# Gathers issued one tile further ahead of the scatter-adds, and a reordered VectorE step, in an attention and expert kernel

## The reference

```python
x = x + xattn(layernorm(x), ctx, Wq, bq, Wk, bk)          # (16, 56, 512), ctx (16, 1500, 512)
# in the expert layer, x is layernorm(x) as 896 rows of 512:
scores = sigmoid(x @ gate_w.T) + bias                     # 16 experts
topk_w, topk_idx = top_k(scores, 4); topk_w /= sum(topk_w)
z  = silu(x @ Wg[e].T) * (x @ Wu[e].T)                    # 256 wide, for each expert
out = sum_e (z * cw[:, e]) @ Wd[e].T + silu(x @ Sg.T) * (x @ Su.T) @ Sd.T
```

## Time and profile before

| | us |
|---|---|
| median of three runs | 559.57 |
| lowest, highest | 557.12, 560.98 |
| the profiled execution's own time | 557.56 |
| its span, first to last instruction | 555.8 |
| busy in it: TensorE matmuls | 487.7 (88%) |
| VectorE, ScalarE, GpSimd | 260.6 (47%), 156.6 (28%), 118.8 (21%) |

### The profile page before, as it was taken

The page is one execution under the profiler, slowest core; times in us unless marked ns, Lnnn a source line. Parts: engine busy times, 40 slices in busy tenths (PEclk is TensorE's granted clock), DMA queues, the critical chain, the costliest instruction groups (busy, mean ns, idle before and its releaser), DMA issues.

```text
span 555.8 us, 10809 instructions
## 1 busy us (share of the span) xinstructions
PE 487.7 (88%) x2472; PEld 297.6 (54%) x2473; DVE 260.6 (47%) x707; ACT 156.6 (28%) x303; POOL 118.8 (21%) x100
## 2 busy tenths in 40 slices
PE   3999999999999999997997935899998889899960
PEld 1583445363636363633475623677766666576740
DVE  3204336273736354544358634354656456654520
ACT  0000302020202020302122431345555456444430
POOL 1000000000000000000002221454554446335531
PEclk9969999999999999998999968799999899899995
DMA  9999999999999999999454654866758677555542
GB/s 216 401 421 423 384 424 418 410 425 401 428 401 426 402 425 403 422 427 404 154 169 97 170 153 153 278 164 149 190 115 214 194 199 180 101 90 93 109 59 36
DMA packets 28231, 149.04 MB, mean 268 GB/s; under 512 B 4072, under 2 KB 4200, under 8 KB 16424
## 3 DMA queue, kind: packets, MB, share of 16 engines
q1 hardware_dynamic: 15832, 123.08, 55.7%
q0 software_dynamic: 8720, 20.21, 20.2%
q10 hardware_dynamic: 3664, 5.57, 3.2%
HBM read 133.84 MB, written 15.01 MB: 268 GB/s over the span
## 4 chain that ended last, share of the span: by engine, by line
PE 66%; DMA 14%; issue 9%; DVE 3%; ACT 2%; DVEq 2%; POOL 2%; POOLq 1%; ACTq 0%; SPq 0%
PE b L571 15%; PE scores L547 15%; PE b L677 14%; DMA taken<-h_rows,take_at 8%; PE b L535 6%; DMA out<-y_sb,add_at 4%; PE b L497 4%; PE scores L677 2%; PE scores L509 2%; PE b L561 2%; DMA w_qk<-in_wk 1%; DVEq L323 1%; PE b L584 1%; PE b L516 1%; ACT probs_t L828 1%
## 5 line engine op out<-in xcount | busy, mean ns | idle before, releaser
L571 PE MATMUL b<-ctx_rows,probs_t 125*64 125x512 f32 (+1 forms) x384 | 86.3, 600 | 0.0
L547 PE MATMUL scores<-ctx_cols,g_t 128*64 128x500 f32 x384 | 84.8, 586 | 0.0
L459 POOL DMA_INDIRECT out<-y_sb,add_at x34 | 53.7, 1579 | 88.3 <-ACT add_at L928 52.6
L423 POOL TENSOR_TENSOR rstd<-var_eps,neg_half 128x1 f32<-128x1 f32 x16 | 8.8, 551 | 268.2 <-DVE var_eps L1019 268.2
L677 PE MATMUL b<-w_hi,taken_hi 128*128 x136 | 57.9, 426 | 1.1 <-ACT taken_hi L905 1.1
L677 PE MATMUL b<-w_lo,taken_hi 128*128 x136 | 56.1, 412 | 0.0
L1277 DVE TENSOR_TENSOR w_lo<-w_raw,w_hi (+1 forms) x33 | 39.7, 1223 | 29.1 <-ACT w_hi L894 29.1
L571 PEld LDWEIGHTS b<-ctx_rows,probs_t 125*64 125x64 f32 (+1 forms) x384 | 26.4, 138 | 48.2 <-issue 47.3
L547 PEld LDWEIGHTS scores<-ctx_cols,g_t 128*64 128x64 f32 x384 | 26.3, 137 | 48.3 <-issue 48.3
L497 PE MATMUL b<-cst,taken 128*128 128x128 f32 x164 | 26.6, 287 | 25.1 <-DMA taken<-h_rows,take_at 24.1
L444 POOL DMA_INDIRECT taken<-h_rows,take_at x34 | 43.1, 1268 | 12.9 <-issue 9.7
(11 more groups left out here) (213 smaller groups left out, 674.1 us busy)
## 6 DMA issues: line engine op xcount, KB each, us to landing
ctx_rows<-in_ctx SPq DMA_DIRECT2D x48, 1024.0 KB, 15.4
ctx_cols<-in_ctx_t SPq DMA_DIRECT2D x32, 1500.0 KB, 18.6
w_raw<-in_experts SPq DMA_DIRECT2D x11, 1536.0 KB, 7.1
h_rows<-h ACTq DMA_DIRECT2D x16, 115.5 KB
taken<-h_rows SPq DMA_DIRECT2D x7, 264.0 KB, 3.0
out<-xs ACTq DMA_DIRECT2D x2, 784.0 KB
shared_raw<-in_shared SPq DMA_DIRECT2D x1, 1536.0 KB, 32.5
xs<-in_x ACTq DMA_DIRECT2D x12, 112.0 KB
```

The lines of the kernel that those rows point to most:

```text
L459: nc.gpsimd.indirect_dma_start(out[:, :], bass.IndirectOffsetOnAxis(ap=add_at[i][:, 0:1], axis=0), y_sb[:, i * DIM:(i + 1) * DIM], None, c ...
L547: last = nc.tensor.matmul(scores[HALF * b:HALF * (b + 1), n, 0:CHUNK], g_t[:, k, HALF * b:HALF * (b + 1)], ctx_cols[:, at:at + CHUNK], sta ...
L571: last = nc.tensor.matmul(b3[HALF * b:HALF * (b + 1), :], probs_t[0:rows_in(p), at:at + HALF], ctx_rows[0:rows_in(p), g, b, c * DIM:(c + 1 ...
```

## The change

GpSimd issues `gather(9)` and `gather(10)` ahead of `add_shared(5)`, `gather(7)` and `gather(8)` ahead of `add_shared(4)`, and in the loop `gather(t+5)` ahead of `add(t)`, where it was `gather(t+4)`. VectorE's step takes the low half, the weight column and the row numbers of coming tiles between `gated_rows` and `z_rows`. TensorE does `ranks` earlier and `lay_tables` later, and VectorE casts `plan` ahead of the fourth shared tile's two gate steps.

```diff
             add_shared(3)
-            add_shared(4)
             pool.wait_ge(init_stored, 16)
             pool.wait_ge(h_stored, PAIRS * 32 + 16)
             pool.wait_ge(plan_ready, 1)
             n_inner = inner_pairs(pool)
             gather(SHARED, 1)
             gather(SHARED + 1, 0)
+            add_shared(4)
+            gather(SHARED + 2, 1)
+            gather(SHARED + 3, 0)
             add_shared(5)
-            gather(SHARED + 2, 1)
+            gather(SHARED + 4, 1)
             add_shared(6)
-            gather(SHARED + 3, 0)
-            with pool.Fori(0, n_inner) as pair:
+            with pool.Fori(0, n_inner - 1) as pair:
                 for k in range(2):
                     t = pair * 2 + (SHARED + k)
-                    gather(t + 4, 1 - k)
+                    gather(t + 5, k)
                     add(t, 1 - k)
-            t = n_inner * 2 + SHARED
-            for k in range(4):
+            t = n_inner * 2 + (SHARED - 2)
+            gather(t + 5, 0)
+            for k in range(6):
                 add(t + k, 1 - k % 2)
...
# TensorE
             up_hi(2, 0, shared_hi, shared_lo, 0)
+            ranks(last_pair)
             z_transpose(1)
             up_lo(2, 0, shared_hi, 0)
             shared_transpose(3)
             down(1, 1, shared_hi, shared_lo, 0)
-            ranks(last_pair)
...
             z_transpose(3)
-            lay_tables()
             up_lo(4, 0, shared_hi, 0)
             shared_transpose(5)
+            lay_tables()
             down(3, 1, shared_hi, shared_lo, 0)
...
# VectorE
             def silu_rows(t, i):
                 gate_rows(t, i)
+                weigh_rows(t, i)
+
+            def weigh_rows(t, i):
                 dve.wait_ge(w_ready, t - (SHARED - 1))
                 settle(dve)
                 dve.wait_ge(gated_ready, t + 1)
...
             pick(last_pair)
+            weigh(last_pair)
             z_to_lo(1)
-            weigh(last_pair)
+            rank_rows(last_pair)
             shared_silu(2)
             taken_to_lo(3)
-            rank_rows(last_pair)
             z_to_lo(2)
...
             enter(last_pair)
+            dve.wait_ge(table_rows_ready, 1)
+            nc.vector.tensor_copy(plan[:], scores[0:1, 2, 0:TABLES * TILES]).then_inc(plan_ready, 1)
             shared_silu(4)
             taken_to_lo(5)
-            dve.wait_ge(table_rows_ready, 1)
-            nc.vector.tensor_copy(plan[:], scores[0:1, 2, 0:TABLES * TILES]).then_inc(plan_ready, 1)
             z_to_lo(4)
...
             def step(t, i):
                 z_to_lo(t - 1)
-                silu_rows(t, i)
+                gate_rows(t, i)
                 taken_to_lo(t + 1)
                 take_weight(t + 1, 1 - i)
                 name_take(t + 3, 1 - i)
+                weigh_rows(t, i)
                 more_thirds(t + 1)
```

## The result

The change makes the kernel slower by 0.9%: 565.69 us (median of 8 runs, 564.04 to 568.89) against 561.21 (8 runs, the three of the table above among them, 557.12 to 569.14), a ratio of 1.0087 with an interval of 1.0046 to 1.0128. Forecast were 534 us. The profiled execution took 565.78 us, 8.2 more than the one before.

A forecast was written before the change was run, and what follows sets the result against it. TensorE was taken to set the pace wherever fed, with late gathers starving it. From 557.6 us profiled, 18.0 for the entry and 6.7 for the loop leave 532.9; as the profiled run lies 2.0 under the median, 534, range 527 to 541.

The forecast's parts named there:

- The entry: Start up to expert tile 11: earlier plan and gathers bring tile 11 18 us earlier, bounds 15 to 21.
- VectorE's new step: no cost, with little cover.: Loop: z_rows ends 2.3 us behind taken_hi, 0.3 us of cover left; cost 0, bounds 0 and 10 us.
- VectorE's order binds: Rival, loop: cover short by 0.3 to 0.5 us in most steps, 10 to 15 us back, 543 to 549; chance 0.13.
- The scatter-adds ... Cost 0: Loop: scatter-adds leave some 2 us later, hidden by 1.3 us before keep_y's need and ScalarE's idle time; cost 0.
- the loop's gain of 6.7: Loop: gathers issued ahead of scatter-adds are seldom late, 6.7 us gained, between 3 and 9.
- this rival: Rival, loop: scatter-adds hold ScalarE, binding over 6.9 us of landing; slower, up to 568 us; chance 0.05.
- the 155 to 160 forecast: Sign, loop: tile 11 to tile 40 would take 155 to 160 us.
- The prediction's own mechanism: GpSimd cannot write descriptors while VectorE holds the port pair; by this each add up to 1.2 us later.

The follow-up runs named there:

- e2: The kernel before with VectorE's new step alone (old GpSimd order, old plan): 573.42 us, ratio 1.0204.
- e12: The change with GpSimd's old loop order (gather t+4, add t), entry and VectorE's new step as changed: 558.37 us, ratio 0.9914.
- e13: The change with only the read of plan for take_at's column moved ahead of gated_rows: 544.84 us, ratio 0.9693.
- e9: The change with VectorE's old step, each expert scatter-add replaced by a one-row store without waits for earlier landings: 527.91 us, ratio 0.9351.
- e3: The kernel before with the change's GpSimd edits alone: 553.62 us, ratio 0.9861.
- e1: The change with VectorE's loop step put back as before, GpSimd's order and earlier plan kept: 549.65 us, ratio 0.9772.
- e5: The change with both of VectorE's reads of plan (weight's and row numbers' column) moved ahead of gated_rows: 543.61 us, ratio 0.9629.
- e8: The change's entry alone, with VectorE's old step and GpSimd's old loop order: 544.14 us, ratio 0.9672.
- e10: The change's entry and new VectorE step, both reads of plan ahead of gated_rows, GpSimd's old loop order: 544.41 us, ratio 0.9673.
- e6: The change with z_rows put ahead of take_at in VectorE's step: 554.96 us, ratio 0.982.
- e11: The change's entry with VectorE's old step, both reads of plan ahead of gated_rows, GpSimd's old loop order: 546.51 us, ratio 0.9683.

## Why the prediction was wrong

**The entry: right.** Forecast were `up_hi` of tiles 7, 8 and 11 at 322.5, 329.6 and 347.5; measured 321.4, 330.8, 349.8. The gain was 15.6 us for 18.0, inside its bounds of 15 to 21. Tile 8 came 1.2 us later than said because the second load, for which I took 7.1 us, needed 8.5 in this chain of waits; the other 1.1 us were lost by tile 11, in steps of 6.1, 6.5 and 6.4 us:

```profile
315.81 8.49 DMA w_raw<-in_experts
```

**The step that failed first: "VectorE's new step: no cost, with little cover."** I had `z_rows` end 2.3 us behind `taken_hi`, against a need of 2.6, and took the end of the range that says 0. Two errors lie in it. The size: with no read held it ends at 2.6 (e2, e12), since between the instructions are 0.1 to 0.3 us of issue that I had not summed. One step of e12, timeline of VectorE and TensorE:

```profile
399.69 0.15 DVE L1303 COPY take_at<-list_at 128x1 int32 x1 [0.68 <-issue]
400.02 0.48 DVE L1324 SCALAR_TENSOR_TENSOR z_rows<-gated_rows,taken_w,b 128x256 f32<-128x256 f32 x1 [0.18 <-issue]
...
400.65 0.41 PE L700 MATMUL b<-cst,z_rows 128*128 128x128 f32 x2
...
402.53 0.63 PE L497 MATMUL b<-cst,taken 128*128 128x128 f32 x4 [0.31 <-issue]
...
406.00 0.48 DVE L1324 SCALAR_TENSOR_TENSOR z_rows<-gated_rows,taken_w,b 128x256 f32<-128x256 f32 x1 [0.18 <-issue]
...
406.63 0.41 PE L700 MATMUL b<-cst,z_rows 128*128 128x128 f32 x2
```

And the argument: I took 0 because a late gather shifts `taken_hi`, `up_hi` and `z_rows` alike. They are chained, but in a ring: `taken_hi` of the next tile stands behind the `z_transpose` that waits for `z_rows`. What the cover lacks is paid in every step, not once. It is also paid with more than it lacks. The cover was short by about 0.1 us, and a step took 5.98 us instead of 5.2. From `z_transpose` to `taken_transpose` it is 402.53 - 400.65 = 1.88 us here, and 388.64 to 389.79, 1.15 us, in the step of the earlier trace rows. TensorE's queue has its own read of `plan` between them in program order, and it is the likely cause; no run moved that read. Before, it did that while the matmuls of `up_hi` still ran, ahead of `z_transpose`; now it stands at `z_transpose` and reads behind it. Users of `plan` in one step, before (`z_transpose` 388.64) and after (508.19):

```profile
L323 PEldq TENSOR_LOAD <-plan x1: 299/299/299, 388.4 to 388.4; - x1
```

```profile
L323 PEldq TENSOR_LOAD <-plan x1: 301/301/301, 509.1 to 509.1; - x1
```

So a round in e12 is 2.6 (`taken_hi` to the end of `z_rows`) + 0.15 + 3.2 (`z_transpose` to the end of `taken_hi`) = 6.0. Where TensorE's read is held, a round is about 6.5. The rival "VectorE's order binds" priced a short cover at 0.3 to 0.5 us a step, 10 to 15 us in all. In the change it is 1.5 in the step shown, and 22 over the loop (189.3 against 167.0 in e13). Its cause was right, its price too low by a third to a half, and its chance of 0.13 too small for a cover of 0.3 us on a sum of small terms.

**What no part of the prediction had: the held read.** Of VectorE's reads of `plan` behind 330 us, 3 of 102 took over 0.36 us before, and 27 of 97 after, 13.8 us over their 0.3 in sum. Twenty of the 27 end 1.7 us behind the end of a scatter-add's issue: the add above ends at 505.09, the read at 506.82. The change has put the add there: GpSimd now issues it behind a gather that waits for `take_at`. The link with the scatter-add holds in all traces. Of all engines' reads behind 330 us in the 13 with scatter-adds, 340 of the 380 that began 0.4 to 1.3 us behind the end of a scatter-add's issue took over 0.36 us, and 83 of the other 2764. With the scatter-adds replaced and all gathers kept (e9), 3 of VectorE's 98 are long. The price of VectorE's held reads in the ring was not measured by itself: at most the 7.3 us (9.7 by the ratios) from e12 to the change. With the read moved out of the ring, held or not, the loop is 22 us shorter (e13).

**The second step that failed: "The scatter-adds ... Cost 0", and with it the loop's gain of 6.7.** I said the add would leave 2 us later. It leaves 4.9 us behind the end of `keep_y` (median 4.5), where it was 1.3. I had counted the gather's issue and a read, not that the gather itself waits for `take_at` (78.5 us of waits above). So `keep_y` finds its buffer not landed: from tile 11 to 40 it waits 9.0 us in the change, 14.6 and 28.0 with the old step (e3, e1), and before it waited for none. I had this rival bind from a landing time of 6.9 us. At a fed pace it is on the edge at the usual 4.8: from the end of one `keep_y` 4.9 + 4.8 = 9.7 us, and the buffer is wanted again after 10.4 - 0.6 = 9.8, so each longer landing is a wait. The change itself is spared part of it by the ring, whose rounds of 6.6 us leave more time. Whether the loop's gathers then help at all: with the ring open, the new loop order gives 543.61 and 544.84 (e5, e13) and the old one 544.14 and 544.41 (e8, e10), no difference that these runs can tell. In the traces one wait takes the place of another: in that part TensorE waits 9.2 us for gathers and `keep_y` not at all for landings in e8; in e13 it is none and 10.4. The gathers also land sooner when they are issued ahead, 3.6 us in the median of e6 (half of them could be timed), 4.4 before. Without scatter-adds the loop takes 158.1 us, within the 155 to 160 forecast. That fits a gain that the later scatter-adds eat, but does not show it, since the old order was not run without them. With VectorE's old step the new order costs outright in the trace of e3 (10.1 us in the loop); e1 against e8 (549.65, 544.14) points the same way, but those intervals overlap.

**A page's rule.** The prediction has gathers held beside a weight subtraction and scatter-adds not. That reading was wrong: the add at 388.35 had begun 0.94 us before its subtraction. The Trainium skill (SBUF — State Buffer, "Who interferes with whom") says that a VectorE instruction with two inputs in SBUF contends with a GpSimd instruction that reads SBUF, and that the one that starts first holds the pair to its end. A weight subtraction has two such inputs, and a gather or scatter-add reads its row numbers there. The traces agree for both. In the change 19 gathers overlap a subtraction, all began first, and all took 0.98 or 0.99 us; in e12 17 began at least 0.05 us behind it, took 1.32 to 2.06, and ended 0.86 to 0.88 behind its end. Three scatter-adds of the change began well inside a subtraction and took 1.72, 2.26 and 2.26 us, ending 1.46 behind its end; none of the others took over 1.59. One of them:

```profile
398.64 1.23 DVE L1279 TENSOR_TENSOR w_lo<-w_raw,w_hi  x1 [1.71 <-issue]
...
399.07 2.26 POOL L459 DMA_INDIRECT out<-y_sb,add_at  x1 [0.95 <-issue]
```

The prediction's own mechanism was the writing of descriptors. The section infers that such a subtraction leaves that alone, and the plain stores of e9, whose issue reads no row numbers, agree: 20 began inside a subtraction and took 0.53 to 0.59 us, where the other 14 took 0.48 to 0.54. In the change all this is 1.5 us of issue in sum, so it was not this that made the scatter-adds late.

**The sum**, forecast -18.0 and -6.7; measured -15.6 for the entry and +24.2 for the loop. Of the 30.9 us between +24.2 and -6.7, the ring with its held reads takes 22.3 (189.3 to 167.0 when one read is moved). The other 8.6, down to 158.4, are what the run without scatter-adds does not have (158.1). Best of all kernels are five that can't be told apart (e5, e8, e10, e11, e13), 543.6 to 546.5 us, 3 to 4% under before: the entry with the old loop order, or the whole change with the column read moved ahead of `gated_rows`.

## What to carry to other kernels

Before a step is put behind others on an engine, ask whether its result feeds, through the other engines, what it now waits for. If so it is a ring: sum every gap in it, reads of registers and 0.1 us of issue included, and compare with the period; a cover of 0.3 us on such a sum is a coin toss, and a shortfall is paid each round. Reads that wait for no other engine's result belong where the engine waits anyway, not between two instructions that others wait for. And where one queue issues both what is wanted early and what frees buffers, moving the first ahead makes the second wait for everything the first waits for.

## What the runs showed of the hardware

- A read of a word of `plan` by an engine's queue takes 0.30 us. When it begins 0.4 to 1.3 us behind the end of a scatter-add's issue it is mostly longer (340 of 380 such reads over 0.36 us, 83 of 2764 others), up to 0.99 us in the change and up to 1.16 in e8, and 329 of those 340 end 0.7 to 1.8 us behind that end. Behind a plain store's issue (e9) 3 of 57 were. All engines' queues have such reads. What on the chip holds them stays open.
- A queue that runs ahead hides its reads and register work. When it has to stand at a wait, that work comes behind the wait: a stretch of 1.15 us on TensorE became 1.88 here. How much of the 0.7 us is the read was not tested.
- The issue of a gather or a scatter-add that begins inside a weight subtraction of VectorE, behind its first 0.05 us and ahead of its last 0.15, ends a fixed time behind the subtraction's end: 0.83 to 0.89 us for gathers (0.98 without one), 1.46 for scatter-adds (1.58 without one), in all traces. When GpSimd begins first, neither is held, and a plain store's issue is not held either (e9).
